# An adaLN feed-forward block: the last product's matmuls cut from 512 to 256 and to 128 columns

## The chip, the core and the metric

The kernel runs on one core of a Trainium2 chip. The metric is the device time of one execution in microseconds (us). The kernel before takes 1260.53 us as a median of two runs (1260.35 and 1260.70).

## The reference

An input x of 32 x 64 x 1024 is first mixed over its 64 channels with one of 16 weight sets, chosen for each sample by `itok`; then a feed-forward layer with 4096 inner columns and a tanh-approximated gelu is added back to x. Everything is float32.

```python
W = weights[condition]
cond = jnp.einsum('bct,bcd->bdt', x, W)
h = jax.nn.gelu(jnp.einsum('bsd,df->bsf', cond, inter_w) + inter_b, approximate=True)
out = x + jnp.einsum('bsf,fd->bsd', h, output_w) + output_b
```

## The kernel before, in words

The 2048 tokens are worked on in two passes of 1024 (index `h`). In each pass both matrix products of the feed-forward layer are done by a Strassen-like scheme: seven block products instead of eight. The first GEMM (`first`, L529 to L567) has eight groups of 14 steps, 112 steps in all. The second GEMM (`second`, L569 to L586) has seven products (index `j`, 0 to 6) of 16 steps each (index `q`), 112 steps too. Every step of either has twelve matmuls. So there are 2 x 112 x 12 = 2688 matmuls of each GEMM.

A step of the second GEMM takes one 128 x 512 block of the inner activations (`lhs`, the stationary operand, four 128 x 128 tiles) and one 128 x 512 block of the output weights (`rhs`, the moving operand). To keep float32 precision in the rounded type float32r, both are split into a high and a low part: ScalarE writes the high parts (L716, L725), VectorE subtracts to get the low ones (L859, L862). For each of four token tiles `tb` three matmuls are then accumulated in one PSUM bank of 512 float32 columns: high x high, high x low, low x high. Each call of `nc.tensor.matmul` names its own stationary tile, and each gets a weight load (LDWEIGHTS) of its own, also where two neighbours name the same tile.

The ring of `lhs` and `rhs` buffers has three slots: ScalarE may write a slot once the step three before has finished (`step_done`), and TensorE waits at each step's start for the low parts (`lhs_lo`, `rhs_lo`). Before the first step of a product, TensorE also waits until VectorE has added the earlier product of the same banks into `acc` (`acc_added`). In the very last step of the program (`h` = 1, `j` = 6, `q` = 15) the last matmul of each of the four tiles signals on its own (`tile_done`); VectorE adds that tile to `acc` (L878), and the DMA queue stores it (L424).

The other matmuls of the program are in plain float32: a warm-up with `ones` (L590), the channel mixing of the two passes (L500 and L517, 128 columns) and one small transposition of the bias (L526, 32 columns). Each such call leaves two loads and two matmuls in the trace, while a float32r call leaves one of each.

Of the kernel before, what the change touches and what calls it, by code (L numbers as in the profile page):

```python
# [12 lines left out]
BANK = 512  # L13
# [14 lines left out]
PRODUCTS = 7  # L28
FRESH = (0, 1, 5)
# [3 lines left out]
def build(nc, x, itok, cond_w, w1, b1, w2, b2, out):  # L33
# [4 lines left out]
    PASSES = 2  # L38
# [5 lines left out]
    PAIRS = 2 * NG  # L44
# [4 lines left out]
    RING = 3  # L49
# [16 lines left out]
    with ExitStack() as ctx:  # L66
        def at(name, kib, shape, dt=F32):
            return nc.alloc_sbuf_tensor_at(name, [P, *shape], dt, offset=BASE + int(kib * KIB))
# [22 lines left out]
        lhs = [at(f"lhs{i}", 160 + 4 * i, [2, BANK], F32R) for i in range(RING)]  # L91
        rhs = [at(f"rhs{i}", 172 + 4 * i, [2, BANK], F32R) for i in range(RING)]
# [17 lines left out]
        ps = ctx.enter_context(nc.psum_tensor("ps", [P, 8, BANK], F32))  # L110
# [62 lines left out]
        def blk(b):  # L173
            return slice(b * P, (b + 1) * P)
# [4 lines left out]
        def step2(h, j, q=0):  # L179
            return h * STEPS + S1STEPS + j * PAIRS + q  # L180

        def rhs_n(h, j, q=0):

            return h * S2STEPS + j * PAIRS + q
# [9 lines left out]
        def bank2(h, j, tb):  # L194
            return 4 * ((ROLE[j] + h) % 2) + tb
# [293 lines left out]
        def _(pe):  # L489
# [79 lines left out]
            def second(h, j, q):  # L569
                s, r = step2(h, j, q), (j * PAIRS + q) % RING  # L570
                pe.wait_ge(lhs_lo, s + 1)
                pe.wait_ge(rhs_lo, rhs_n(h, j, q) + 1)
                for tb in range(TB):
                    if q == 0 and j >= 2 and tb % 2 == 0:
                        pe.wait_ge(acc_added, (h * PRODUCTS + j - 2) * 2 + tb // 2 + 1)
                    if q == 0 and j < 2 and tb == 0:
                        pe.wait_ge(c21_gelu, 2 * (h * NG + NG - 1 + j))
                        pe.wait_ge(c11_added, 2 * (h * NG + NG - 1 + j))
                    for u, (a, w) in enumerate(((0, 0), (0, 1), (1, 0))):
                        last = nc.tensor.matmul(ps[:, bank2(h, j, tb), :], lhs[s % RING][:, a, blk(tb)], rhs[r][:, w, :],  # L580
                                                start=(j in FRESH and q == 0 and u == 0),
                                                stop=(q == PAIRS - 1 and u == 2), skip_group_check=True)
                    if step2(h, j, q) == PASSES * STEPS - 1:
                        last.then_inc(tile_done, 1)
                if step2(h, j, q) < PASSES * STEPS - 1:
                    last.then_inc(step_done, 1)  # L586
# [7 lines left out]
            for h in range(PASSES):  # L594
                for g in range(NG):
                    for c in range(CHUNKS):
                        first(h, g, c)
                        if (h, g, c) == (0, 0, 0):
                            turn_b1()
                        if (h, g) == (0, 0):  # L600
                            for j in range(TILES):
                                if BEHIND[j] == c:
                                    cond1(j)
                for j in range(PRODUCTS):
                    for q in range(PAIRS):
                        second(h, j, q)
# [386 lines left out]
```

## Time and profile before

| what | value |
|---|---|
| median of two runs | 1260.53 us |
| profiled execution, its time | 1260.64 us |
| profiled execution, its span | 1258.8 us |
| TensorE busy (PE) | 1253.7 us, 5664 matmuls |
| weight loads (PEld) | 1043.1 us, 5664 loads |
| VectorE busy (DVE) | 825.6 us |
| ScalarE busy (ACT) | 566.9 us |

"Busy" is the time that is covered by at least one record of the engine. Matmul records overlap: each lasts longer than the distance to the next one, and their ends are modelled. The distance from one matmul's start to the next is therefore read from a stretch of time and the number of matmuls in it, not from the mean duration of a record.

### The profile page before, as it was taken

The page shows a single profiled execution, that of the slowest core. Times are in us where ns is not written, and L with a number is a line of the kernel's source. Part 1 is how long each engine was busy: PE and PEld are TensorE (multiplying, and loading weights), DVE is VectorE, ACT ScalarE, POOL GpSimd, SP SyncE. Part 2 cuts the span into 40 slices and gives each one's busy share as a digit, 9 for nine tenths or more (in the row PEclk, how much of TensorE's full clock was granted, in tenths as well). Part 3 has the DMA queues.
Part 4 walks back from the last instruction along what each step waited for, and adds up shares of the span by engine and source line. Part 5 has one row for each costly group of instructions (what it writes and reads, how often), then busy time and mean ns, then how long its engine had stood idle before and what let it go on. Part 6 is the DMA issues. An engine that isn't in the chain of part 4 may idle for free.

```text
span 1258.8 us, 15370 instructions
## 1 busy us (share of the span) xinstructions
PE 1253.7 (100%) x5664; PEld 1043.1 (83%) x5664; DVE 825.6 (66%) x1087; ACT 566.9 (45%) x969; POOL 188.1 (15%) x95
## 2 busy tenths in 40 slices
PE   9999999999999999999999999999999999999998
PEld 9888888888888888888888888888888888888887
DVE  5977787676577777657655455554547767784764
ACT  4845454454544444444434444444444444444442
POOL 4362223321000000000034233312200000000000
PEclk9999999999999999999999999999999999999999
DMA  9586655764997322349835224544189932223431
GB/s 343 160 275 244 242 196 222 283 250 177 384 392 283 97 89 99 101 165 360 310 137 195 95 119 174 184 184 145 74 330 396 351 132 93 101 101 100 155 131 51
DMA packets 94090, 249.28 MB, mean 198 GB/s; under 512 B 7328, under 2 KB 15552, under 8 KB 92608
## 3 DMA queue, kind: packets, MB, share of 16 engines
q1 hardware_dynamic: 93408, 248.14, 54.6%
q8 instruction: 46, 0.75, 0.2%
q14 instruction: 28, 0.23, 0.1%
q10 hardware_dynamic: 576, 0.15, 0.1%
q0 software_dynamic: 32, 0.00, 0.0%
HBM read 162.28 MB, written 85.98 MB: 197 GB/s over the span
## 4 chain that ended last, share of the span: by engine, by line
PE 97%; DVE 1%; DMA 1%; SPq 0%; POOL 0%; ACT 0%; issue 0%; ACTq 0%; DVEq 0%
PE ps L580 48%; PE ps L564 48%; DMA w_raw<-in_L_ffn_inter_w_dram 1%; PE ps L517 1%; POOL s_w L476 0%; SPq L321 0%; DVE y_whole L795 0%; DVE acc L878 0%; DVE lhs L800 0%; DVE y_whole L782 0%; DVE y L789 0%; SPq L318 0%; ACT lhs L646 0%; ACT y_stage L623 0%; SPq L317 0%
## 5 line engine op out<-in xcount | busy, mean ns | idle before, releaser
L564 PE MATMUL ps<-y,lhs 128*128 128x512 f32 x2688 | 611.4, 389 | 0.0
L580 PE MATMUL ps<-rhs,lhs 128*128 128x512 f32 x2688 | 609.6, 389 | 0.0
L580 PEld LDWEIGHTS ps<-rhs,lhs 128*128 128x128 f32 x2688 | 504.7, 188 | 104.6
L564 PEld LDWEIGHTS ps<-y,lhs 128*128 128x128 f32 x2688 | 504.2, 188 | 104.3
L716 ACT ACTIVATE lhs<-h_raw 128x512 fp32r<-128x512 f32 x224 | 141.6, 632 | 345.8 <-PE ps L580 340.2
L859 DVE TENSOR_TENSOR lhs<-h_raw,lhs 128x512 fp32r<-128x512 f32 x224 | 155.0, 692 | 188.5 <-ACT lhs L716 188.5
L800 DVE TENSOR_TENSOR lhs<-w_raw,lhs 128x512 fp32r<-128x512 f32 x128 | 111.1, 870 | 131.6 <-ACT lhs L646 131.5
L646 ACT ACTIVATE lhs<-w_raw 128x512 fp32r<-128x512 f32 x128 | 80.9, 633 | 171.7 <-PE ps L564 165.2
L862 DVE TENSOR_TENSOR rhs<-W,rhs 128x512 fp32r<-128x512 f32 x224 | 153.3, 684 | 0.0
L800 DVE TENSOR_TENSOR lhs<-s_w,lhs 128x512 fp32r<-128x512 f32 x96 | 91.3, 953 | 89.3 <-ACT lhs L646 89.1
L468 POOL TENSOR_TENSOR s_w<-w_raw 128x1024 f32<-128x1024 f32 x16 | 48.9, 3055 | 620.3 <-PE ps L580 354.0
L725 ACT ACTIVATE rhs<-W 128x512 fp32r<-128x512 f32 x224 | 137.9, 616 | 0.0
L646 ACT ACTIVATE lhs<-s_w 128x512 fp32r<-128x512 f32 x96 | 60.6, 632 | 125.1 <-PE ps L564 119.9
L891 DVE TENSOR_TENSOR W<-W,W 128x512 f32<-128x512 f32 x128 | 87.5, 684 | 0.0
L655 ACT ACTIVATE c<-c,b_col 128x512 f32<-128x512 f32 x96 | 68.2, 710 | 4.8 <-DVE c L807 4.8
L807 DVE TENSOR_TENSOR c<-ps,c 128x512 f32<-128x512 f32 x96 | 65.5, 682 | 0.0
L652 ACT ACTIVATE c<-ps 128x512 f32<-128x512 f32 x96 | 56.1, 584 | 5.5 <-DMA h_mem<-c 5.5
L476 POOL TENSOR_TENSOR s_w<-s_w,w_raw 128x1024 f32<-128x1024 f32 x16 | 41.9, 2620 | 37.0 <-DVE lhs L800 36.5
L484 POOL TENSOR_TENSOR s_w<-w_raw,s_w 128x1024 f32<-128x1024 f32 x16 | 41.4, 2588 | 39.1 <-DVE lhs L800 38.4
L485 POOL TENSOR_TENSOR w_raw<-w_raw 128x1024 f32<-128x1024 f32 x16 | 46.2, 2885 | 0.0
L814 DVE TENSOR_TENSOR hs<-c,c 128x1024 f32<-128x1024 f32 x32 | 40.5, 1267 | 0.0
L878 DVE TENSOR_TENSOR acc<-ps,acc 128x1024 f32<-128x1024 f32 (+1 forms) x30 | 34.3, 1146 | 4.2 <-PE ps L580 4.2
(38 smaller groups left out, 290.1 us busy)
## 6 DMA issues: line engine op xcount, KB each, us to landing
h_raw<-h_mem SPq DMA_DIRECT2D x112, 512.0 KB, 3.3
w_raw<-in_L_ffn_inter_w_dram SPq DMA_DIRECT2D x32, 1024.0 KB, 8.6
h_mem<-hs SPq DMA_DIRECT2D x64, 512.0 KB, 4.5
W<-in_L_ffn_output_w_dram SPq DMA_DIRECT2D x32, 1024.0 KB, 12.4
h_mem<-c SPq DMA_DIRECT2D x48, 512.0 KB, 5.4
y_mem<-y_out SPq DMA_DIRECT2D x28, 512.0 KB, 3.5
y<-y_mem SPq DMA_DIRECT2D x7, 2048.0 KB, 12.8
acc<-in_x_dram SPq DMA_DIRECT2D x16, 512.0 KB, 9.0
```

The lines of the kernel that those rows point to most:

```text
L564: last = nc.tensor.matmul(ps[:, bank, :], w[:, k, :], y[i][:, part, k, :], start=(i in FRESH and k == 0 and u == 0), stop=(k == KH - 1 and ...
L580: last = nc.tensor.matmul(ps[:, bank2(h, j, tb), :], lhs[s % RING][:, a, blk(tb)], rhs[r][:, w, :], start=(j in FRESH and q == 0 and u == ...
L646: nc.scalar.activation(split1(s, 0), w1_part(h, g, c), ACT.Copy).then_inc(lhs_hi, 1)
L652: nc.scalar.activation(to[:, p, :], ps[:, bank1(h, g, role, p), :], ACT.Copy).then_inc(copied, 1)
L655: nc.scalar.activation(tile[:, p, :], of, ACT.Gelu_apprx_tanh, bias=b1_col[:, 4 * g + 2 * m + p:4 * g + 2 * m + p + 1]).then_inc(made, 1)
L716: nc.scalar.activation(lhs[s % RING][:, 0, :], of, ACT.Copy).then_inc(lhs_hi, 1)
L725: nc.scalar.activation(rhs[r][:, 0, :], w2_part(j, q), ACT.Copy).then_inc(rhs_hi, 1)
L800: nc.vector.tensor_tensor(split1(s, 1), w1_part(h, g, c), split1(s, 0).bitcast(F32), ALU.subtract).then_inc(lhs_lo, 1)
L807: nc.vector.tensor_tensor(tile[:, p, :], ps[:, bank, :], tile[:, p, :], ALU.add).then_inc(added, 1)
L859: nc.vector.tensor_tensor(lhs[s % RING][:, 1, :], of, lhs[s % RING][:, 0, :].bitcast(F32), ALU.subtract).then_inc(lhs_lo, 1)
L862: nc.vector.tensor_tensor(rhs[r][:, 1, :], w2_part(j, q), rhs[r][:, 0, :].bitcast(F32), ALU.subtract).then_inc(rhs_lo, 1)
L891: nc.vector.tensor_tensor(to[:, pair], a[:, pair], b[:, pair], ALU.subtract).then_inc(t_made[n], 1)
```

## The change

Only the loop around the matmul call of `second` is changed. In the seventh product (`j` = 6) of the second pass, which is the last product of the program, every matmul of 512 columns becomes two of 256 columns in steps 0 to 7, and four of 128 columns in steps 8 to 15. All other products keep one matmul of 512 columns.

```diff
+                    width = BANK if (h, j) != (PASSES - 1, PRODUCTS - 1) else BANK // 2 if q < PAIRS // 2 else BANK // 4
                     for u, (a, w) in enumerate(((0, 0), (0, 1), (1, 0))):
-                        last = nc.tensor.matmul(ps[:, bank2(h, j, tb), :], lhs[s % RING][:, a, blk(tb)], rhs[r][:, w, :],
-                                                start=(j in FRESH and q == 0 and u == 0),
-                                                stop=(q == PAIRS - 1 and u == 2), skip_group_check=True)
+                        for n in range(0, BANK, width):
+                            cols = slice(n, n + width)
+                            last = nc.tensor.matmul(ps[:, bank2(h, j, tb), cols], lhs[s % RING][:, a, blk(tb)], rhs[r][:, w, cols],
+                                                    start=(j in FRESH and q == 0 and u == 0),
+                                                    stop=(q == PAIRS - 1 and u == 2), skip_group_check=True)
```

The two places on TensorE follow; in each row stand the line, the operand buffers, the output's shape and a count, and `waits` names the semaphores in front of the matmul. Before, the end of product 5 and the first steps of product 6 in the second pass:

```order
L580 MATMUL ps<-rhs2_85,lhs2_82 128x512 x11
L580 MATMUL ps<-rhs0_83,lhs0_80 128x512 [waits acc_added,rhs_lo,lhs_lo]
L580 MATMUL ps<-rhs0_83,lhs0_80 128x512 x5
L580 MATMUL ps<-rhs0_83,lhs0_80 128x512 [waits acc_added]
L580 MATMUL ps<-rhs0_83,lhs0_80 128x512 x5
L580 MATMUL ps<-rhs1_84,lhs1_81 128x512 [waits rhs_lo,lhs_lo]
L580 MATMUL ps<-rhs1_84,lhs1_81 128x512 x11
```

And the same place with the change:

```order
L583 MATMUL ps<-rhs2_85,lhs2_82 128x512 x11
L583 MATMUL ps<-rhs0_83,lhs0_80 128x256 [waits acc_added,rhs_lo,lhs_lo]
L583 MATMUL ps<-rhs0_83,lhs0_80 128x256 x11
L583 MATMUL ps<-rhs0_83,lhs0_80 128x256 [waits acc_added]
L583 MATMUL ps<-rhs0_83,lhs0_80 128x256 x11
L583 MATMUL ps<-rhs1_84,lhs1_81 128x256 [waits rhs_lo,lhs_lo]
L583 MATMUL ps<-rhs1_84,lhs1_81 128x256 x23
```

No wait has moved; behind each there are twice as many matmuls of half the width. The second place is the middle of product 6, where step 7 hands over to step 8, with the change:

```order
L583 MATMUL ps<-rhs1_84,lhs1_81 128x256 [waits rhs_lo,lhs_lo]
L583 MATMUL ps<-rhs1_84,lhs1_81 128x256 x23
L583 MATMUL ps<-rhs2_85,lhs2_82 128x128 [waits rhs_lo,lhs_lo]
L583 MATMUL ps<-rhs2_85,lhs2_82 128x128 x47
L583 MATMUL ps<-rhs0_83,lhs0_80 128x128 [waits rhs_lo,lhs_lo]
L583 MATMUL ps<-rhs0_83,lhs0_80 128x128 x47
```

From step 8 on a step has 48 matmuls of 128 columns where it had twelve of 512. The order of the work of the other engines and of the DMA queue is the same.

## Rows read from the trace of the kernel before

**Rows 1.** The page's head: span, and each engine's busy time.

```profile
span 1258.8 us, 15370 instructions
PE 1253.7 (100%) x5664; PEld 1043.1 (83%) x5664; DVE 825.6 (66%) x1087; ACT 566.9 (45%) x969; POOL 188.1 (15%) x95
```

**Rows 2.** The chain that ended last, from 950 us on: start, us, what.

```profile
950.87 302.61 PE ps L580 x1335
1253.49 0.02 issue
1253.51 2.73 DVE acc L878 x4
```

**Rows 3.** Busy time of each engine by stretch, last product's time; granted clock behind POOL.

```profile
1210.00:1240.00 30.00, 30.00 (x134) 24.84 (x133) 17.18 (x26) 12.78 (x23) 0.00 (x0) 1.00 0.33 105
```

**Rows 4.** TensorE's groups with shapes apart: busy us, mean ns, idle before.

```profile
L580 PE MATMUL ps<-rhs,lhs 128*128 128x512 f32 x2688 | 609.6, 389 | 0.0
L517 PE MATMUL ps<-wdiag,x 128*128 128x128 f32 x128 | 15.2, 275 | 0.4 <-ACT y_stage L623 0.4
L526 PE MATMUL ps<-ident,b_rows 32*128 32x32 f32 x2 | 0.4, 282 | 0.0
...
L580 PEld LDWEIGHTS ps<-rhs,lhs 128*128 128x128 f32 x2688 | 504.7, 188 | 104.6
L517 PEld LDWEIGHTS ps<-wdiag,x 128*128 128x128 f32 x128 | 15.0, 192 | 1.1 <-issue 0.8
L526 PEld LDWEIGHTS ps<-ident,b_rows 32*128 32x128 f32 x2 | 0.3, 182 | 0.4 <-issue 0.4
```

**Rows 5.** Timeline of TensorE's matmuls, 46.2 to 49.2 us: start, us, what.

```profile
46.04 3.40 PE L517 MATMUL ps<-wdiag,x 128*128 128x128 f32 x29
```

**Rows 6.** Timeline of the weight loads, 46.2 to 49.2 us.

```profile
46.04 3.32 PEld L517 LDWEIGHTS ps<-wdiag,x 128*128 128x128 f32 x29
```

**Rows 7.** Timeline of the weight loads, 23.9 to 24.2 us.

```profile
23.99 0.29 PEld L526 LDWEIGHTS ps<-ident,b_rows 32*128 32x128 f32 x2 [0.35 <-issue]
```

**Rows 8.** Timeline of the weight loads, 24.40 to 24.50 us.

```profile
24.32 0.30 PEld L564 LDWEIGHTS ps<-y,lhs 128*128 128x128 f32 x2
```

**Rows 9.** Timeline of all engines in one step of the last product, 1220 to 1223 us.

```profile
1220.19 0.63 ACT L716 ACTIVATE lhs<-h_raw 128x512 fp32r<-128x512 f32 x1 [1.56 <-PE ps L580]
1220.73 0.62 ACT L725 ACTIVATE rhs<-W 128x512 fp32r<-128x512 f32 x1
1220.86 0.69 DVE L859 TENSOR_TENSOR lhs<-h_raw,lhs 128x512 fp32r<-128x512 f32 x1 [1.43 <-ACT lhs L716]
1221.46 0.68 DVE L862 TENSOR_TENSOR rhs<-W,rhs 128x512 fp32r<-128x512 f32 x1
```

**Rows 10.** Timeline of all engines at the end, 1252.5 us on.

```profile
1252.18 3.33 PE L580 MATMUL ps<-rhs,lhs 128*128 128x512 f32 x14
1254.23 2.37 SPq L424 DMA_DIRECT2D out_dram<-acc  x4
```

## The prediction

> **What bounds the kernel now.** I read the page's head first, then the chain that ended last, then the busy times of the stretch that is changed, and then single loads and matmuls. The head [rows 1] shows TensorE (PE) covered for 1253.7 of 1258.8 us, with VectorE at 66% and ScalarE at 45%. The chain [rows 2] says what that cover is made of: from 950.87 us on, 1335 matmuls of the second GEMM take 302.61 us without a wait between them, so one follows the other every 302.61 / 1335 = 0.2267 us. Only 2.73 us of VectorE's additions come after. In the stretch of the last product [rows 3] TensorE is busy for 30.00 of 30.00 us at a granted clock of 1.00, which is the 2.4 GHz level. So whatever one matmul of this product costs more is added to the time one for one.
>
> The other engines keep up with ease. In a step of the last product, ScalarE works 0.63 + 0.62 us and VectorE 0.69 + 0.68 us [rows 9], while TensorE needs 12 x 0.2267 = 2.72 us. ScalarE waits for TensorE 1.56 us in each step, not the other way round. A longer step on TensorE makes these waits longer and delays nobody else.
>
> **What is in 0.2267 us.** At 2.4 GHz, 512 columns at one per cycle are 213.3 ns, so 13.3 ns are left over per matmul. The load of the next weights is hidden: its record lasts 188 ns [rows 4] and does not show in the distance. The question of this change is what remains when the columns get fewer while each matmul still brings a load of 128 x 128 weights.
>
> **How close two loads can come.** No float32r matmul narrower than 512 is in the trace. I look for loads that had little work beside them. The small float32 transposition of 32 columns [rows 7] has two loads that together span 0.29 us, at 0.18 us each [rows 4], so the second began 0.29 - 0.18 = 0.11 us after the first; yet its matmul's 32 columns need far less than that (32 / 2.4 = 13 ns per run through the array). The next step of the first GEMM begins with the array empty: its first two loads, which are float32r weights, span 0.30 us at 0.19 us each [rows 8], again 0.11 us apart. And where 128-column float32 matmuls follow one another, 29 loads span 3.32 us [rows 6], or (3.32 - 0.19) / 28 = 0.112 us from load to load, and 29 matmuls span 3.40 us [rows 5], or (3.40 - 0.28) / 28 = 0.112 us. So 0.11 us is the shortest distance that I see between two loads, with 32 columns beside them or with more. I read it as what a load takes before the next can begin.
>
> The Trainium skill ("TensorE: Matmul & The Clock Gate", section "LDWEIGHTS (loading the stationary operand)") gives a load as its columns divided by 1.2 GHz, which for 128 columns is 107 ns. The 0.11 us of rows 7 and 8 agree with it. An estimate by that page alone, 384 loads of 107 ns in the narrow half, would make that half 41 us and the sum 19 us for it instead of the 21 us below.
>
> **The change, part by part.** It removes 192 matmuls of 512 columns (16 steps x 12) with 192 loads, that is 192 x 0.2267 = 43.52 us, half of it (21.76 us) in each half of the product.
>
> - *Steps 0 to 7, 256 columns:* 96 x 2 = 192 matmuls with 192 loads. The columns take 256 / 2.4 = 106.7 ns, and I leave the 13.3 ns on top: 0.120 us each, 23.04 us in all, **+1.3 us**. The load's 0.11 us just fits beneath. The bounds: 0.112 us [rows 5], if the gap shrinks with the width (-0.3 us for the half), and 0.188 us, if a load's whole record were in the way (36.1 us, +14.3 us). I take 0.120, since the gap is that of the same type of matmul.
> - *Steps 8 to 15, 128 columns:* 96 x 4 = 384 matmuls with 384 loads. The columns take only 53.3 ns, less than the 0.11 us between loads, so the loads set the pace. The bounds are wide: below, columns plus gap, 53.3 + 13.3 = 66.7 ns (25.6 us, +3.8 us); above, the price of a float32 matmul of the same shape, which is two loads and two matmuls, 2 x 0.112 = 0.223 us (85.7 us, +64.0 us), or four times the columns with the gap, 0.2267 us (87.0 us, +65.3 us). I take the row that is nearest, the distance from load to load of 128-column matmuls, 0.1117 us: 384 x 0.1117 = 42.9 us, **+21.1 us**.
> - *The end of the program:* VectorE's four last additions follow the four tiles one by one [rows 2], 0.68 us each. Before, a tile's twelve matmuls take 2.72 us / 4 = 0.68 us as well; now 48 / 4 x 0.1117 = 1.34 us, so each addition is done before the next tile is, and behind the last matmul there stays one addition and its store, as before [rows 10]. Nothing is gained or lost here beyond 0.2 us.
> - *Signals, waits, transfers:* none is added or moved. The matmuls behind each wait are more, and what is queued behind them has slack [rows 9].
>
> Sum: 1.3 + 21.1 = **+22.4 us**. The profiled execution took 1260.64 us, 0.11 us more than the median of the runs shown, and so the forecast is **1283 us**, 1.8% above before. A gain is all but excluded: the columns are the same, and if every gap of 13.3 ns in this product vanished, 192 x 13.3 = 2.6 us would be won.
>
> **The rivals.**
>
> - *The gap stands on the load too.* If the 13.3 ns come with the change of weights and not with the columns, a narrow matmul costs 106.7 + 13.3 = 120 ns, and the sum is 576 x 0.120 - 43.52 = +25.6 us: 1286 us, just over 2%. For it: the gap of the 512-column matmul, 13.3 ns, is larger than that of the float32 ones, whose 0.1117 us hold two runs of 128 columns, 106.7 ns, and 5 ns more. Against it: two float32r loads in rows 8 are 0.11 us apart.
> - *Narrow float32r runs like float32.* If a float32r matmul below some width costs what a float32 one does, four runs per column, 128 columns cost 0.223 to 0.227 us and the half +64 to +65 us. With +1.3 us for 256 columns that gives 1326 to 1327 us, slower by 5%. It decides from a narrow price of about 0.119 us on, where the sum passes 2%. For it: the only rows of 128 columns that exist are float32 and take exactly that [rows 4, 5], and nothing shows that the one-run form holds for narrow ones. Against it: float32 shows two records per call, and the change issues the same type as before. If 256 columns fell into it as well (0.44 us each), it would be 1388 us.
> - *The load's record lies bare.* 0.188 us per narrow matmul: +50.4 us, and 1312 to 1325 us with the 256-column half free or not. Against it: in rows 6 loads of 0.192 us follow each other every 0.112 us.
> - *The clock falls.* With columns in the array for less than half of the last 43 us, the granted clock could drop to 1.2 GHz, the loads would take twice as long, and the narrow half would cost about +64 us as in the second rival. Against it: the clock is 1.00 in the stretch before [rows 3], and TensorE would have no pause.
> - *The loads do not bind.* Then 66.7 ns per narrow matmul and +5.1 us in all: 1266 us. Against it stand rows 6 to 8. The Trainium skill ("TensorE: Matmul & The Clock Gate", section "Back-to-back issue gap") gives 81 ns for pairs of a load and a 128-column matmul; by that rule the narrow half would take 384 x 81 ns = 31.1 us, and the whole would come to +10.6 us. The rows at 0.112 us do not bear it out for 4-byte weights, so this rival and that rule share one small chance.
>
> **How the numbers follow.** The loads set the pace at 128 columns, with 0.60: 0.48 for a pace that stays under 2%, 0.12 for the 120 ns of the first rival or a little more. Narrow float32r like float32: 0.20, of it 0.17 for 128 columns alone. The bare record: 0.06. The clock: 0.04. The loads do not bind: 0.07. Something else, or no change in effect: 0.03. Two per cent is 25.2 us, about what a measurement of this kernel can tell from no change. Within 2%: 0.48 + 0.07 + 0.02 = 0.57. Slower: 0.12 + 0.20 + 0.06 + 0.04 = 0.42. Faster: 0.01.
>
> The likeliest case alone spans 1279 us (0.107 us per narrow matmul, the float32 distance without its 5 ns, and 0.112 us per 256-column one: 41.1 + 21.5 - 43.5 = +19.1 us) to 1287 us. That holds 0.60, so the range must reach to the rivals on the slow side, up to 1328 us: 0.60 + 0.17 + 0.06 + 0.04 = 0.87. Left out are the loads that do not bind, 256 columns at the float32 price, and the rest.
>
> **What would show it.** In the changed kernel's trace, 192 matmuls of 128 x 256 should follow each other every 0.120 us (a step of 2.88 us) and 384 of 128 x 128 every 0.112 us (a step of 5.36 us), with the loads as dense as the matmuls, and the granted clock at 1.00 to the end. Two records per narrow call, or steps of over 10 us, would show the float32 price; steps of 3.2 us, that loads do not bind. ScalarE's wait in each narrow step should grow by about 2.6 us, and the end behind the last matmul should be as long as before. I am wrong if the load of float32r weights is faster than the rows here show, or if a float32r matmul's price per column depends on its width.

## The result, and the profile after

The changed kernel takes 1283.49 us (two runs, 1283.32 and 1283.65) against 1260.53 us before: a ratio of 1.0177, with a 95% interval of 1.0161 to 1.0194. It is slower by 23.0 us; 22.4 us were forecast.

The page's head of the changed kernel, which answers to [rows 1]:

```profile
span 1281.8 us, 16138 instructions
PE 1276.1 (100%) x6048; PEld 1072.8 (84%) x6048; DVE 829.8 (65%) x1087; ACT 567.0 (44%) x969; POOL 186.6 (15%) x95
```

TensorE's groups of the second GEMM in the changed kernel, shapes apart (busy us, mean ns), which answer to [rows 4]:

```profile
L583 PE MATMUL ps<-rhs,lhs 128*128 128x512 f32 x2496 | 566.1, 389 | 0.0
L583 PE MATMUL ps<-rhs,lhs 128*128 128x128 f32 x384 | 43.0, 274 | 0.0
L583 PE MATMUL ps<-rhs,lhs 128*128 128x256 f32 x192 | 23.2, 283 | 0.0
```

The chain that ended last in the changed kernel (start, us, what), which answers to [rows 2]:

```profile
951.59 327.00 PE ps L583 x1728
1278.59 0.02 issue
1278.62 0.69 DVE acc L881
```

There are 384 more matmuls and 384 more loads, one record of each per call: the narrow float32r matmul has not turned into a float32 one. The whole second GEMM of the last pass is still one piece without a wait: 327.00 us. Of its 1728 matmuls 1152 are of 512 columns, 1152 x 0.2267 = 261.1 us, so the last product takes 65.9 us, where it took 43.5. The sum of the prediction had 23.04 + 42.89 = 65.93 us.

The changed kernel's timeline of matmuls, in a stretch of 256 columns and in one of 128 (start, us, what):

```profile
1217.82 14.44 PE L583 MATMUL ps<-rhs,lhs 128*128 128x256 f32 x119
...
1239.78 30.43 PE L583 MATMUL ps<-rhs,lhs 128*128 128x128 f32 x271
```

And its timeline of the loads in the same stretches:

```profile
1217.83 14.35 PEld L583 LDWEIGHTS ps<-rhs,lhs 128*128 128x128 f32 x119
...
1239.83 30.34 PEld L583 LDWEIGHTS ps<-rhs,lhs 128*128 128x128 f32 x271
```

The distance from start to start is the piece's length less one record, divided by the count less one: (14.44 - 0.283) / 118 = 0.1200 us at 256 columns, and (30.43 - 0.274) / 270 = 0.1117 us at 128. There are as many loads as matmuls, at the same distances. The same stretches as busy times, with the granted clock behind POOL:

```profile
1216.00:1232.00 16.00, 16.00 (x136) 16.00 (x135) 8.90 (x13) 6.55 (x12) 0.00 (x0) 1.00 0.51 165
1240.00:1272.00 32.00, 32.00 (x289) 32.00 (x289) 6.46 (x10) 5.78 (x10) 0.00 (x0) 1.00 0.00 1
```

Loads are busy all the time now, where they left 17% free in [rows 3]; the clock stays at 1.00, the 2.4 GHz level.

One step of the narrow half, and the end of the program, in the changed kernel's timeline of all engines:

```profile
1241.09 0.63 ACT L719 ACTIVATE lhs<-h_raw 128x512 fp32r<-128x512 f32 x1 [4.16 <-PE ps L583]
...
1246.45 0.63 ACT L719 ACTIVATE lhs<-h_raw 128x512 fp32r<-128x512 f32 x1 [4.21 <-PE ps L583]
...
1269.81 8.76 PE L583 MATMUL ps<-rhs,lhs 128*128 128x128 f32 x77
...
1277.28 0.69 DVE L881 TENSOR_TENSOR acc<-ps,acc 128x512 f32<-128x512 f32 x1 [0.65 <-PE ps L583]
1278.62 0.69 DVE L881 TENSOR_TENSOR acc<-ps,acc 128x512 f32<-128x512 f32 x1 [0.65 <-PE ps L583]
```

A step lasts 1246.45 - 1241.09 = 5.36 us, and ScalarE's wait in it grew from 1.56 us [rows 9] to 4.2 us. The last matmul's record ends at 1269.81 + 8.76 = 1278.57 us and the last addition at 1279.31 us, 0.74 us later. Before, it was 1256.24 - 1255.51 = 0.73 us [rows 2, 10].

### The profile page after: what moved, and what is told of

It is laid out like the page before. It is cut to its first block, busy times and chain, and to the rows that moved or that the text cites. A ratio compares the mean times of both kernels' runs of the same rounds, so it can differ in the third digit from the quotient of the medians.

```text
span 1281.8 us, 16138 instructions
## 1 busy us (share of the span) xinstructions
PE 1276.1 (100%) x6048; PEld 1072.8 (84%) x6048; DVE 829.8 (65%) x1087; ACT 567.0 (44%) x969; POOL 186.6 (15%) x95
## 4 chain that ended last, share of the span: by engine, by line
PE 97%; DVE 1%; DMA 1%; SPq 0%; ACT 0%; issue 0%; ACTq 0%; DVEq 0%
PE ps L583 49%; PE ps L564 47%; DMA w_raw<-in_L_ffn_inter_w_dram 1%; PE ps L517 1%; DVE y_whole L798 1%; SPq L321 0%; DVE lhs L803 0%; DVE y_whole L785 0%; DVE y L792 0%; ACT lhs L649 0%; ACT y_stage L626 0%; SPq L317 0%; DVE acc L881 0%; SPq L318 0%; SPq L319 0%
## 5 line engine op out<-in xcount | busy, mean ns | idle before, releaser
L583 PE MATMUL ps<-rhs,lhs 128*128 128x512 f32 (+2 forms) x3072 | 632.0, 368 | 0.0
L583 PEld LDWEIGHTS ps<-rhs,lhs 128*128 128x128 f32 x3072 | 534.5, 188 | 97.4
L803 DVE TENSOR_TENSOR lhs<-w_raw,lhs 128x512 fp32r<-128x512 f32 x128 | 115.1, 901 | 127.1 <-ACT lhs L649 127.0
L485 POOL TENSOR_TENSOR w_raw<-w_raw 128x1024 f32<-128x1024 f32 x16 | 46.2, 2890 | 0.0
```

The source lines that it names most:

```text
L583: last = nc.tensor.matmul(ps[:, bank2(h, j, tb), cols], lhs[s % RING][:, a, blk(tb)], rhs[r][:, w, cols], start=(j in FRESH and q == 0 and ...
L803: nc.vector.tensor_tensor(split1(s, 1), w1_part(h, g, c), split1(s, 0).bitcast(F32), ALU.subtract).then_inc(lhs_lo, 1)
```

## The experiments

The theory: one matmul with its load costs the larger of its columns at 2.4 GHz with a gap, and of 0.1117 us for the load. The rival that the result leaves standing: a float32r column costs double below some width, whatever the load, since 128 x 2 / 2.4 + 5 ns is 0.1117 us as well. Each edit is against the changed kernel; each diff shows its new lines without the old `width` line, and `...` stands for lines left out. Apart from the two kernels with one half each, every kernel ran once, beside the kernel before on the same chip: 1261.0 us (a median of 15), 1261.4 and 1261.35 us in the three groups. Runs of one kernel lie up to 2.6 us apart, so the distances in the traces decide, and not differences of 1 us.

**Each half alone.** Two kernels, with the 256-column half and with the 128-column half:

```diff
+ width = BANK // 2 if (h, j) == (PASSES - 1, PRODUCTS - 1) and q < PAIRS // 2 else BANK
```
```diff
+ width = BANK // 4 if (h, j) == (PASSES - 1, PRODUCTS - 1) and q >= PAIRS // 2 else BANK
```

> The 256-column half of the change alone: steps 0 to 7 of the last product in 192 matmuls of 256 columns, steps 8 to 15 as before. The load theory (one matmul costs the larger of its columns at 2.4 GHz plus 13.3 ns, and of 0.1117 us for its load): 0.120 us from matmul to matmul, 192 x 0.120 - 21.76 = +1.3 us, 1261.8 us, with the ratio just above 1.001. The width theory (a float32r column below some width costs double, whatever the load): the same at 256 if the limit is below it, +20 us or more if 256 is already narrow.

> The 128-column half alone: steps 8 to 15 in 384 matmuls of 128 columns, steps 0 to 7 as before. Both theories: 0.1117 us from matmul to matmul, 384 x 0.1117 - 21.76 = +21.1 us, 1281.6 us; with the 256-column half's price it should add up to the whole change. If the change of width between the halves cost something of its own, the sum of the two halves would miss the whole by more than 1 us.

Measured: 1262.7 us (ratio 1.0014, 1.0005 to 1.0023) and 1282.5 us (1.0173, 1.0159 to 1.0187), against 1261.0 us. So 256 columns cost 1.7 us, 128 columns 21.5 us, together 23.2 us where the whole change cost 23.0: the halves add up, and the change of width between them costs nothing that can be seen. In the traces of the two kernels the distances are 0.1200 and 0.1117 us again. Theory and rival both allow this.

**Fewer columns, the same load.**

```diff
+ width = BANK // 8 if (h, j) == (PASSES - 1, PRODUCTS - 1) and q >= PAIRS // 2 else BANK
```

> Steps 8 to 15 in 768 matmuls of 64 columns, the rest as before. The load theory: a load still takes 0.1117 us, so matmul follows matmul at that distance as with 128 columns: 768 x 0.1117 - 21.76 = +64.0 us, 1324.5 us. The width theory (two cycles per column): 64 x 2 / 2.4 + 5 = 58 ns, 768 x 0.058 - 21.76 = +23 us, 1283.6 us, about the same as with 128 columns.

Measured: 1398.42 us, +137 us, which neither expected. Busy times by stretch in that kernel (granted clock behind POOL):

```profile
1238.00:1241.00 3.00, 3.00 (x30) 3.00 (x29) 0.00 (x0) 0.00 (x0) 0.00 (x0) 1.00 0.02 5
1241.00:1243.00 2.00, 2.00 (x13) 2.00 (x12) 0.00 (x0) 0.00 (x0) 0.00 (x0) 0.54 0.00 0
1243.00:1244.00 1.00, 1.00 (x6) 1.00 (x7) 0.00 (x0) 0.00 (x0) 0.00 (x0) 0.50 0.00 0
```

Its timeline of matmuls, in a stretch before the clock fell and in one after:

```profile
1236.30 4.41 PE L583 MATMUL ps<-rhs,lhs 128*128 128x64 f32 x38
...
1299.71 40.51 PE L583 MATMUL ps<-rhs,lhs 128*128 128x64 f32 x189
```

Two things happened. As long as the granted clock was 1.00, matmuls of 64 columns followed each other every (4.41 - 0.28) / 37 = 0.112 us, the same as with 128 columns; that is the load theory, and the rival's 58 ns is out. Then, at about 1241 us, the granted clock fell to 0.50 (1.2 GHz) and stayed there to the end, though TensorE shows busy for the whole of each stretch. What it did before the fall was one matmul of 64 columns every 0.112 us. At 1.2 GHz the distance is (40.51 - 0.39) / 188 = 0.2134 us. Taken as the load alone, that is 0.2134 x 1.2 = 256 cycles for 128 float32r columns, two per column, and at 2.4 GHz 106.7 of the 111.7 ns; a fixed time within both distances would make it somewhat less, and no run separates the two. This kernel ran once, and what sets off the fall of the clock no run here isolates. (The 0.28 and 0.39 us taken off are one record's duration, 274 ns at the full clock in the next kernel and 392 ns as this one's mean.)

**The same 64 columns, in short stretches.**

```diff
+ width = BANK // 8 if (h, j) == (PASSES - 1, PRODUCTS - 1) and q >= PAIRS // 2 and tb == 0 else BANK
```

> In steps 8 to 15 only the first of the four token tiles is done in matmuls of 64 columns (24 per step, 192 in all), the other three tiles and steps 0 to 7 in matmuls of 512, so that no long stretch of narrow matmuls arises. The load theory: the granted clock stays at 1.00 and each narrow matmul costs 0.1117 us, 192 x 0.1117 - 24 x 0.2267 = +16.0 us, 1276.5 us. Rival, that 64 columns by themselves cost what the all-64 kernel showed after its clock had fallen (0.2133 us): 192 x 0.2133 - 5.4 = +35.5 us, 1296 us. The width theory (58 ns): +5.7 us, 1266 us.

Measured: 1277.92 us, +16.5 us (1261.4 us before). Its group of narrow matmuls (busy us, mean ns):

```profile
L583 PE MATMUL ps<-rhs,lhs 128*128 128x64 f32 x192 | 22.1, 274 | 0.0
```

Its busy times over steps 8 to 15 (granted clock behind POOL):

```profile
1234.00:1276.00 42.00, 38.79 (x268) 35.31 (x266) 10.61 (x17) 6.90 (x12) 0.00 (x0) 0.99 0.07 26
```

The 0.99 takes in the 3.2 us after the last matmul (TensorE is busy for 38.79 of the 42 us); from 1234 to 1270 us the granted clock is 1.00. With three tiles of 512 columns between the narrow ones, nine matmuls in each step, the clock holds, and 192 matmuls of 64 columns cost what 192 of 128 would. Load theory and size are both met; what the all-64 kernel lost beyond its +64 us was the clock.

**Half the load, the same columns.**

```diff
+ width = BANK // 4 if (h, j) == (PASSES - 1, PRODUCTS - 1) and q >= PAIRS // 2 else BANK
+ some = P // 2 if (h, j) == (PASSES - 1, PRODUCTS - 1) and q >= PAIRS // 2 else P
- last = nc.tensor.matmul(ps[:, bank2(h, j, tb), cols], lhs[s % RING][:, a, blk(tb)], rhs[r][:, w, cols],
+ last = nc.tensor.matmul(ps[0:some, bank2(h, j, tb), cols], lhs[s % RING][:, a, tb * P:tb * P + some], rhs[r][:, w, cols],
```

> Steps 8 to 15 in 384 matmuls of 128 columns as in the change, but each with only 64 of the 128 stationary columns: half of each weight load, and half of the tokens of these steps are left out of the sums. Steps 0 to 7 as before. The load theory, if a load's time goes by its columns: the load falls to about 0.056 us and the columns with their gap bind, 53.3 + 13.3 = 66.7 ns, 384 x 0.0667 - 21.76 = +3.8 us, 1264.4 us. The width theory, and a load whose time does not go by its columns: 0.1117 us as before, +21.1 us, 1281.6 us.

Measured: 1263.12 us, +2.1 us. Its groups of matmuls and of loads in these steps:

```profile
L584 PE MATMUL ps<-rhs,lhs 128*64 128x128 f32 x384 | 23.2, 222 | 0.0
...
L584 PEld LDWEIGHTS ps<-rhs,lhs 128*64 128x64 f32 x384 | 23.2, 134 | 0.1
```

Its timeline of matmuls in these steps:

```profile
1237.82 16.36 PE L584 MATMUL ps<-rhs,lhs 128*64 128x128 f32 x270
```

The matmuls have the same 128 columns, and with half the stationary columns they follow each other every (16.36 - 0.222) / 269 = 0.0600 us. So the 0.1117 us was the load's, and with half of its columns it takes no more than 0.0600 us; how much less cannot be seen, since 53.3 ns of it are the moving columns. The rival on width is refuted a second time. (Half of the output's rows are gone as well, but at 512 columns that saves nothing, as shown below.) The expected 66.7 ns was too much by 6.7: the gap above the columns was 6.7 ns here, not 13.3.

**Operands of two bytes.**

```diff
+ width = BANK // 4 if (h, j) == (PASSES - 1, PRODUCTS - 1) and q >= PAIRS // 2 else BANK
...
+ if (h, j) == (PASSES - 1, PRODUCTS - 1) and q >= PAIRS // 2:
+     stationary, moving = stationary.bitcast(mybir.dt.bfloat16)[:, 1::2], moving.bitcast(mybir.dt.bfloat16)[:, 1::2]
...
```

> Steps 8 to 15 in 384 matmuls of 128 columns as in the change, but with both operands read as bfloat16 (the upper half of each float32r word, at a stride of two), so that these steps are computed with fewer bits; steps 0 to 7 as before. If a load takes its time by its 128 columns whatever their type: 0.1117 us from matmul to matmul and +21.1 us, 1281.6 us. If it is the 4-byte weights that make it slow: the columns bind, 53.3 ns and a gap of 2.5 to 13.3 ns, 384 x 0.056 to 0.067 - 21.76 = -0.3 to +3.8 us, 1260.2 to 1264.4 us.

Measured: 1261.45 us, against 1261.4 us before. Its groups of matmuls and of loads in these steps:

```profile
L588 PE MATMUL ps<-rhs,lhs 128*128 128x128 bf16 x384 | 22.2, 218 | 0.0
...
L588 PEld LDWEIGHTS ps<-rhs,lhs 128*128 128x128 bf16 x384 | 22.0, 97 | 0.3 <-issue 0.3
```

Its timeline of matmuls in these steps:

```profile
1237.82 16.39 PE L588 MATMUL ps<-rhs,lhs 128*128 128x128 bf16 x283
```

(16.39 - 0.218) / 282 = 0.0573 us from matmul to matmul: 53.3 ns of columns and 4 ns. A load of 128 bfloat16 columns hides beneath 128 columns. Both operands changed their type here, but moving float32r columns alone are not slow: with half a load they followed each other every 0.0600 us. So the penalty of narrow matmuls is that of four-byte weights. The Trainium skill ("TensorE: Matmul & The Clock Gate", section "Weight-path perf modes — Fast Weight Load (FWL) and DoubleRow") has a faster way of loading 128 weights that are not float32. These rows agree in that bfloat16 loads need at most 0.0573 us and float32r loads 0.1117 us; whether the bfloat16 loads went that way they do not show.

**Uneven pieces.**

```diff
+ pieces = ((0, BANK),) if not ((h, j) == (PASSES - 1, PRODUCTS - 1)) else ((0, 192), (192, 320)) if q < PAIRS // 2 else ((0, 384), (384, 128))
- for n in range(0, BANK, width):
+ for n, width in pieces:
```

> The last product's matmuls in uneven pieces: 192 and 320 columns in steps 0 to 7, 384 and 128 in steps 8 to 15. The load theory gives each piece the larger of columns / 2.4 + 13.3 ns and 0.1117 us: 0.1117, 0.1467, 0.1733 and 0.1117 us. Per 512 columns that is 0.2583 and 0.2850 us where 0.2267 were, 96 x 0.0317 + 96 x 0.0583 = +8.6 us, 1269.1 us. The width theory (double below 256): the 192-column piece costs 192 x 2 / 2.4 + 5 = 0.165 us, and the sum is +13.7 us, 1274.3 us.

Measured: 1270.36 us, +9.0 us (1261.4 us before), where the load theory said +8.6 and the rival +13.7. Its timeline in steps 0 to 7, where pieces of 320 and 192 columns take turns (the row begins and ends with one of 320):

```profile
1214.70 15.59 PE L583 MATMUL ps<-rhs,lhs 128*128 128x320 f32 x119
```

A pair takes (15.59 - 0.333) / 59 = 0.2586 us, as the load theory has it (0.2583); double columns for the 192 would make it 0.165 + 0.1467 = 0.312 us. What each piece of a pair takes by itself is argued and not shown: their records do not start at the distances that the theory gives them one by one (the one of 320 starts only 0.09 us after the one of 192).

**Where the 13.3 ns come from.** Two kernels with half of the stationary columns, at 512 columns in steps 8 to 15 and at 256 in steps 0 to 7:

```diff
+ width = BANK
+ some = P // 2 if (h, j) == (PASSES - 1, PRODUCTS - 1) and q >= PAIRS // 2 else P
...
```
```diff
+ width = BANK // 2 if (h, j) == (PASSES - 1, PRODUCTS - 1) and q < PAIRS // 2 else BANK
+ some = P // 2 if (h, j) == (PASSES - 1, PRODUCTS - 1) and q < PAIRS // 2 else P
...
```

> Matmuls of 512 columns throughout, as before, but in steps 8 to 15 of the last product each with only 64 of its 128 stationary columns (half of the tokens of these steps are left out of the sums). It asks where the 13.3 ns above the columns come from. If the gap goes by the load: 213.3 + 6.7 = 220 ns from matmul to matmul, 96 x -0.0067 = -0.6 us. If it belongs to the moving columns or to the matmul: 226.7 ns as before, 0 us.

> Steps 0 to 7 in matmuls of 256 columns as in the change, but each with 64 of the 128 stationary columns (half of the tokens of these steps are left out of the sums); steps 8 to 15 of 512 columns as before. It asks what the 13.3 ns above the columns are at 256 columns. If they belong to the matmul, as at 512 columns: 120 ns from matmul to matmul, +1.3 us. If the load with its own gap is what binds at 256 too: half a load, and 106.7 + 6.7 = 113.3 ns as in the 128-column kernel with half loads (60.0 = 53.3 + 6.7 ns), 0.0 us.

Measured: 1261.4 us against 1261.4, and 1262.36 us against 1261.35. The times say nothing at this size; the timelines of matmuls do. At 512 columns:

```profile
1235.67 18.56 PE L584 MATMUL ps<-rhs,lhs 128*64 128x512 f32 x80
```

At 256 columns:

```profile
1215.75 14.44 PE L584 MATMUL ps<-rhs,lhs 128*64 128x256 f32 x126
```

At 512 columns the distance is (18.56 - 0.39) / 79 = 0.2300 us, 3 ns more than with a whole load; at 256 it is (14.44 - 0.276) / 125 = 0.1133 us, 6.7 ns less. So at 256 columns the gap went down with the load, although half a load is far from binding there; at 512 it did not. I have no account that fits both. This stays open.

**The rival of the float32 price, made on purpose.**

```diff
+ width = BANK // 4 if (h, j) == (PASSES - 1, PRODUCTS - 1) and q >= PAIRS // 2 else BANK
+ as_type = (lambda of: of.bitcast(F32)) if (h, j) == (PASSES - 1, PRODUCTS - 1) and q >= PAIRS // 2 else (lambda of: of)
...
```

> The second rival made on purpose: steps 8 to 15 in 384 calls of 128 columns with both operands read as plain float32, steps 0 to 7 of 512 columns as before. Each call should leave two loads and two matmuls, 2 x 0.1117 = 0.2233 us, 384 x 0.2233 - 21.76 = +64.0 us, 1325.4 us, with the granted clock at 1.00 since each load has 256 cycles of columns beside it. If plain float32 cost the same as the narrow float32r of the change: +21.1 us, 1282.5 us.

Measured: 1324.3 us, +63 us (1261.35 us before). Its group of these matmuls:

```profile
L584 PE MATMUL ps<-rhs,lhs 128*128 128x128 f32 x768 | 85.9, 275 | 0.0
```

Its timeline in these steps:

```profile
1249.81 60.46 PE L584 MATMUL ps<-rhs,lhs 128*128 128x128 f32 x540
```

Twice as many records as calls, (60.46 - 0.275) / 539 = 0.1117 us each. This is what the second rival would have looked like: the narrow float32r call of the change costs half of a float32 one, and it leaves one load and one matmul where the float32 call leaves two of each. The granted clock was 1.00 from 1240 to 1318 us; the reason that was given for it, the columns beside each load, is not shown by this run.

No version that beats the kernel before came out of this: at full precision every narrower cut that was run costs time, and none saves any.

## Why the prediction was right, point by point

- *What bounds it:* right. TensorE has no wait in the changed product, and all of its extra time is in the total.
- *Steps 0 to 7, 0.120 us each, +1.3 us:* 0.1200 us in the trace; alone the half measured +1.7 us with an interval of +0.6 to +2.9 us (0.05% to 0.23% of 1261 us). The reason given, columns and a fixed gap, is only half supported: with half a load the gap at 256 columns was 6.7 ns, so part of it goes with the load. The size was right all the same.
- *Steps 8 to 15, 0.1117 us each, +21.1 us:* 0.1117 us in the trace, +21.5 us alone. The step that carried it was reading two loads beside little work [rows 7, 8] as the time that a load needs; cutting the columns again and halving the load showed it. The third digit holds some luck: rows 7 and 8 give the distance only to 0.01 us, which is 3.8 us over 384 matmuls. The 0.1117 us came from plain float32 rows [rows 5, 6], where a load and two runs of 128 columns would each fill the same time, and no run shows which of them sets the pace there.
- *The end, waits and transfers at nothing:* 0.74 us behind the last matmul against 0.73 before, and no engine behind. One slip changes nothing: twelve matmuls are a step of before, not a tile, which had three; the 0.68 us are right.
- *The first rival, the gap on top of the load (120 ns at 128 columns):* it did not come at 128 columns, where 0.1117 us leaves no room for it; its 1286 us were 2.5 us too high.
- *Narrow float32r like float32:* did not come. It was given 0.20 because no row of before had a narrow float32r matmul; the two loads of each float32 call were the hint against it.
- *The bare load record:* 0.188 us did not come. *The loads do not bind:* did not come either; 66.7 ns would have needed a load that is faster than 0.11 us, as the bfloat16 one is.
- *The falling clock:* not at 128 columns, where it stays at 1.00. It is no empty fear, though: at 64 columns it came, and cost 73 us more than the loads did.

Forecast and result differ by 0.5 us. The chain of the changed product begins 951.59 - 950.87 = 0.7 us later than before, so a difference of that size lies ahead of the change.

## What to carry to other kernels

Here a matmul cost about the larger of its moving columns and its weight load, and the load was hidden only as long as the columns lasted longer. A float32r load of 128 columns took about as long as 256 moving columns, so 256 was nearly free, and each halving below it about doubled the price of a column. Where a profile has no row of the narrow case, look for two loads with little work between them: their distance was the floor here. And before cutting further, look at the granted clock, since an engine that shows busy throughout can still be given the lower one.

## What the runs showed of the hardware that was not expected

- In one run the clock fell with TensorE shown busy for 100% of the time and without a pause: in a stretch of 64-column matmuls at 0.112 us each, back to back, the granted clock went from 1.00 to 0.50 and stayed there. With the same narrow matmuls in stretches of 24, and nine of 512 columns between them, it stayed at 1.00.
- The load of float32r weights slows with the array's clock: 0.1117 us from matmul to matmul at 2.4 GHz, 0.2134 us at 1.2 GHz, where the load sets the pace.
- A bfloat16 matmul of 128 columns with its load costs 0.0573 us, about half of the float32r one (0.1117 us).
- The gap between matmuls is not one constant: 13.3 ns at 512 and 256 columns with a whole load, 16.7 and 6.7 ns with half a load, 6.7 ns at 128 columns with half a load.
